# A state space block with adapters and experts on one Trainium2 core: the first additions of the states' products move from VectorE and GpSimd to two accumulating DMAs, and jobs change their places

## The reference

```python
h = x @ cond_W.T + b + 2 * (x @ A[idx]) @ Bm[idx]                    # cond: dense layer with an adapter
u, gate = split(h @ W_in.T)                                          # 2048 channels each
u = silu(causal_conv(u, 4 taps) + conv_b)
dt, Bm, Cm = split(u @ Wx.T, [64, 16, 16]); each rmsnorm * weight    # xp, ms
delta = softplus(dt @ Wdt.T + dt_bias)                               # dt
for t in tokens:                                                     # 2048 channels x 16 states
    state = exp(delta[t] * A) * state + delta[t] * u[t] * B[t]
    y[t] = sum_n state[n] * C[t][n]
x1 = x + ((y + u * D) * silu(gate)) @ W_out.T
h2 = x1 @ base_W.T + base_b + adapter2(x1)
w = top-2 softmax of h2 @ gate_w.T over 8 experts of rank 64
out = x1 + sum_e w_e * (h2 @ lora_A[e].T) @ lora_B[e].T
```

## Time and profile before

| | |
|---|---|
| median of 3 runs | 2556.78 us |
| the profiled execution | 2555.34 us, span 2553.6 us |
| PE busy | 2273.3 us (89%) |
| DVE busy | 2234.1 us (87%) |
| POOL busy | 2121.3 us (83%) |
| ACT busy | 1620.3 us (63%) |
| chain that ended last | PE 51%, DVE 22%, ACT 12%, issue 7%, POOL 7% |
| DMA | 350.05 MB, 137 GB/s in the mean, queue of SP 36.1% of 16 engines' span, of ACT 6.0% |

### The profile page before, as it was taken

One profiled execution on the slowest core, in us unless ns is written; L12 is line 12 of the kernel. 1 busy time (PEld: TensorE's weight loads), 2 busy tenths in 40 slices (PEclk: granted clock), 3 DMA queues, 4 the chain that ended last, 5 costly groups with the idle time before them and its releaser, 6 DMA issues.

```text
span 2553.6 us, 30492 instructions
## 1 busy us (share of the span) xinstructions
PE 2273.3 (89%) x10128; PEld 1918.1 (75%) x10128; DVE 2234.1 (87%) x2098; ACT 1620.3 (63%) x3768; POOL 2121.3 (83%) x1092
## 2 busy tenths in 40 slices
PE   7978898899879997999889997899978978787878
PEld 6867786688768886788768886788867766666767
DVE  1369797899989998999989998999989999999892
ACT  1367566776577766775667665776667765776550
POOL 0088787899889998999979998999979998999880
PEclk9989999899899998999999998999989998888989
DMA  6363443444345433544445433544426332432332
GB/s 209 125 212 100 115 142 119 151 142 139 119 171 155 140 133 105 197 149 140 125 142 168 148 126 116 177 160 136 135 70 215 116 108 91 169 120 90 116 104 89
DMA packets 132250, 350.05 MB, mean 137 GB/s; under 512 B 38573, under 2 KB 43181, under 8 KB 130621
## 3 DMA queue, kind: packets, MB, share of 16 engines
q1 hardware_dynamic: 109326, 296.19, 36.1%
q10 hardware_dynamic: 22768, 51.93, 6.0%
HBM read 337.04 MB, written 11.02 MB: 136 GB/s over the span
## 4 chain that ended last, share of the span: by engine, by line
PE 51%; DVE 22%; ACT 12%; issue 7%; POOL 7%; ACTq 1%; DMA 0%; SPq 0%; DVEq 0%; POOLq 0%
DVE scan L1241 12%; PE late L666 11%; PE ubank L584 10%; PE ubank L613 9%; ACT scan L1076 7%; DVE st L1253 5%; PE gbank L566 5%; POOL st L1464 3%; POOL st L1472 2%; PE scan L584 2%; PE small L640 2%; DVE ubank L1222 2%; PE gbank L630 2%; PE scan L566 1%; ACT ubank L937 1%
## 5 line engine op out<-in xcount | busy, mean ns | idle before, releaser
L1464 POOL TENSOR_TENSOR st<-w_sb,bc 128x1024 f32<-128x1024 f32 x512 | 1198.1, 2355 | 163.5 <-PE gbank L630 150.2
L1241 DVE TENSOR_TENSOR_SCAN scan<-scan,st 128x1024 f32<-128x1024 f32 x512 | 1156.5, 2285 | 40.1 <-POOL st L1464 22.7
L1076 ACT ACTIVATE scan<-delta,A_sb 128x255 f32<-128x255 f32 x2048 | 846.2, 459 | 0.0
L1472 POOL TENSOR_TENSOR st<-st 128x1024 f32<-128x1024 f32 x256 | 603.1, 2356 | 73.1 <-DVE st L1253 63.0
L584 PE MATMUL ubank<-h,wt 128*128 128x256 f32 x1712 | 445.2, 419 | 130.5 <-ACT qg L1155 125.7
L613 PE MATMUL ubank<-h,wt 128*128 128x256 f32 x2048 | 481.6, 390 | 41.5 <-ACT qg L1155 36.3
L584 PEld LDWEIGHTS ubank<-h,wt 128*128 128x128 f32 x1712 | 360.1, 213 | 208.4 <-ACT qg L1155 150.6
L1073 ACT ACTIVATE scan<-iota 128x4 f32<-128x4 f32 x512 | 86.8, 170 | 655.0 <-DVE st L1253 631.6
L613 PEld LDWEIGHTS ubank<-h,wt 128*128 128x128 f32 x2048 | 400.4, 196 | 103.7 <-ACT qg L1155 40.9
L1253 DVE TENSOR_TENSOR st<-scan,bc 128x1024 f32<-128x1024 f32 x384 | 453.7, 1207 | 0.0
L666 PE MATMUL late<-yg,wt 128*128 128x256 f32 x1792 | 410.5, 388 | 32.6 <-DVE x L1278 29.6
(11 more groups left out here) (217 smaller groups left out, 2253.8 us busy)
## 6 DMA issues: line engine op xcount, KB each, us to landing
wt<-in_W_in SPq DMA_DIRECT2D x256, 512.0 KB, 3.6
wt<-in_W_out SPq DMA_DIRECT2D x128, 512.0 KB, 3.4
wt<-in_cond_W SPq DMA_DIRECT2D x64, 512.0 KB, 3.6
bc<-bc_rows ACTq DMA_DIRECT2D x64, 512.0 KB, 6.6
wt<-G_tiles SPq DMA_DIRECT2D x32, 512.0 KB, 3.6
wt<-in_ffn_B SPq DMA_DIRECT2D x26, 512.0 KB, 3.4
xb<-in_x SPq DMA_DIRECT2D x8, 1024.0 KB, 5.6
x<-in_x ACTq DMA_DIRECT2D x28, 256.0 KB, 3.9
```

What stands on the lines that cost most here:

```text
L1076: last = fn(t[:, k, 1:T], delta[:, c, 1:T], ACT.Exp, scale=A_sb[:, col:col + 1])
L1241: v_.tensor_tensor_scan(Tps[q % 2][:, :], Tps[q % 2][:, :], x_, 0.0, ALU.mult, ALU.add).then_inc(scan_done, 1)
L1464: tt(st[:, n % ST_RING, :, :], w_sb[:, i % 2:i % 2 + 1, :].to_broadcast([P, NQ, T]), bc[:, 0, q * NQ:(q + 1) * NQ, :], ALU.mult).then_inc( ...
L1472: tt(st[:, n % ST_RING, :, :], st[:, n % ST_RING, :, :], st[:, (n - 1) % ST_RING, :, :], ALU.add).then_inc(add_done, 1)
```

## The change

It has two parts. In the first, quarter 1's product goes into the ring like the others, and POOL issues two DMAs that add: plane 1 += plane 0 as soon as the product of q = 1 is done, and plane 2 += plane 1 when that has landed and the product of q = 2 is done. POOL then adds plane 3 to plane 2 and folds as before. add_first is gone from DVE and one add from POOL. The ring has seven planes.

```diff
-ST_RING = 6
+ST_RING = 7
@@ vector
-                if q == 1:
-                    v_.tensor_tensor(Tps[1][:, :], Tps[1][:, :], cq, ALU.mult).then_inc(prod_done, 1)
-                else:
-                    v_.tensor_tensor(plane(n), Tps[q % 2][:, :], cq, ALU.mult).then_inc(mul_done, 1)
-
-            def add_first(i):
-                dve.wait_ge(prod_done, i + 1)
-                dve.wait_ge(mul_done, 4 * i + 1)
-                v_.tensor_tensor(plane(4 * i + 1), Tps[1][:, :], plane(4 * i), ALU.add).then_inc(mul_done, 1)
+                v_.tensor_tensor(plane(n), Tps[q % 2][:, :], cq, ALU.mult).then_inc(mul_done, 1)
@@ gpsimd
-                if q == 2 and i:
-                    pool.wait_ge(mul_done, 4 * i - 2)
-                if q == 1 and i >= 2:
+                if q == 2 and i >= 2:
                     pool.wait_ge(id_mm, i - 1)
+                if q == 3 and i:
+                    pool.wait_ge(acc_st[0], 16 * i)
+            def add_dma(i, k):
+                n = 4 * i + k
+                pool.wait_ge(mul_done, n + 1)
+                if k == 2:
+                    pool.wait_ge(acc_st[0], 16 * (i + 1))
+                pool.dma_start(st[:, n % ST_RING, :, :], st[:, (n - 1) % ST_RING, :, :], accum_op=ALU.add
+                               ).then_inc(acc_st[k - 1], 16)
@@ gpsimd, the loop over the chunks
+                last = i + 1 == CHUNKS
+                add_dma(i, 1)
                 for b, j in softplus_of(i - 1):
                     delta_add(b, j)
-                if i + 1 < CHUNKS:
+                if not last:
                     weight(i + 1)
-                    for q in range(3):
-                        dbu(i + 1, q)
-                add(i, 2)
+                    dbu(i + 1, 0)
+                    dbu(i + 1, 1)
+                add_dma(i, 2)
+                if not last:
+                    dbu(i + 1, 2)
+                    dbu(i + 1, 3)
                 add(i, 3)
                 fold(i)
-                if i + 1 < CHUNKS:
-                    dbu(i + 1, 3)
```

```diff
@@ u_chunks
-        if c <= 5:
+        if c <= 4:
             return [NC + 2 * (c - 1), NC + 2 * c - 1]
@@ half_job
-    if j < B and c in (1, 3, 5, 7, 8, 9):
-        return ("cond", j, {1: 0, 3: 1, 5: 2, 7: 4, 8: 5, 9: 7}[c])
+    if j < B and c in (3, 5, 7, 8, 9, 11):
+        return ("cond", j, {3: 0, 5: 1, 7: 2, 8: 3, 9: 5, 11: 7}[c])
@@ tensor
-                        for v in u_chunks(5):
+                        for v in u_chunks(4):
                             pe.wait_ge(u_done, v + 1)
...
                 ubank_free(i)
+                if small_job(i) and small_job(i)[0] == "xp":
+                    x_proj(small_job(i), range(NC - 1 if i >= NC else NC - 2, NC))
@@ scalar
                 fn_exp_table()
                 if i == 0:
-                    for m in range(4, KH):
-                        pro_cond(1, m)
+                    pro_cond(1, 4)
...
                     decay(i + 1, 0)
...
+                if i == 0:
+                    pro_cond(1, 5)
```

More of the change, by code:

```diff
@@ L103, in small_job @@
         return ("dt", b, c + 3)
-    if c in (6, 9) and j < B:
-        return ("cond", j, {6: 3, 9: 6}[c])
+    if c == 9 and j < B:
+        return ("cond", j, 4)
     if c in (10, 11):
         return (("lg", "wT")[c - 10], f, 0)
-    if c in (14, 15):
+    if b == LAST and c in (14, 15):
         return ("B", f, {14: 3, 15: 2}[c])
@@ L157, in takes_half @@
 def takes_half(i):
-    return late_job(i) if late_job(i) and late_job(i)[0] in ("g", "b2", "bias") else half_job(i)
+    if late_job(i) and late_job(i)[0] in ("g", "b2"):
+        return late_job(i)
+    return small_job(i) if small_job(i) and small_job(i)[0] == "bias" else half_job(i)
 def job_tiles(job):
@@ L362, in build @@
         scan_done = sem("scan_done")
-        prod_done = sem("prod_done")
         mul_done = sem("mul_done")
         add_done = sem("add_done")
+        acc_st = [sem(f"acc_st{i}") for i in range(2)]
         id_mm = sem("id_mm")
@@ L592, in h0_ready @@
                 else:
-                    pe.wait_ge(*emptied(("cond", b, 6)))
-                    pe.wait_ge(*emptied(("cond", b, 7)))
+                    for m in (4, 6, 7):
+                        pe.wait_ge(*emptied(("cond", b, m)))
             def ubank_free(i):
@@ L631, in sum_states, with x_proj @@
                 last.then_inc(id_mm, 1)
-            def x_proj(job):
+            def x_proj(job, cs):
                 b = job[1]
-                pe.wait_ge(u_done, NC * (b + 1))
-                for c in range(NC):
+                pe.wait_ge(u_done, NC * b + cs[-1] + 1)
+                for c in cs:
                     n = TILE_NO[("wx", b, c // 8)]
@@ L641, in x_proj @@
                               start=(c == 0), stop=(c == NC - 1))
-                last.then_inc(done_inc(job), 1)
+                if cs[-1] == NC - 1:
+                    last.then_inc(done_inc(job), 1)
             def mean_square(job):
@@ L721, in weights_b @@
             def weights_b(m, o):
-                return mm(o, sel[:, m * P:(m + 1) * P], wT[:, :], start=True, stop=True)
+                for e in range(2):
+                    pick = ident[0:E, 2 * m + e:2 * m + e + 1].to_broadcast([E, ER])
+                    last = mm(o[e * ER:(e + 1) * ER, :], pick, wT[:, :], start=True, stop=True)
+                return last
             def expert_out(f, m, o):
@@ L751, in run @@
                 elif kind == "xp":
-                    x_proj(job)
+                    x_proj(job, range(NC - 1 if i % NC == 12 and i >= NC else NC - 2))
                 elif kind == "ms":
```

137 lines of the change are left out of this document (71 added, 66 removed).

## The result

The changed kernel takes 2579.11 us, the median of 4 runs (2575.76 to 2580.49), against 2556.28 of the kernel before on the same chip: 1.009 times, with a 95% interval of 1.0072 to 1.0109. It is slower by 0.9%, where 2505 was forecast. The profiled executions have spans of 2578.7 and 2553.6 us, 25.1 apart.

What follows compares the result with a forecast made beforehand. Steady slots (first scan to next chunk's first scan, 17.56 us) were taken as bound by DVE, ACT, DVE, plus holes. 0 + 12 - 38 - 11 - 6.5 - 4 - 5 = -52.5 from 2556.78 gave 2505 us, range 2470 to 2650.

Steps and rivals of the forecast that it cites:

- part 2: GpSimd's add becomes two accumulating DMAs: its loop averages 17.35 us, under the 17.56 of a steady slot, so 0.
- part 3: Last slots and tail: GpSimd's longer loop and the last chunk's landing cost +12 us (ends 0 and +25).
- Part 1: The first add leaves DVE: it lies in ACT's shadow, so 0; the taps' wait on ACT becomes 1.5 us.
- Rival C: DVE's add does count, as the taps get their u chunk earlier; floor 2465 us; chance 0.08.
- e: Time POOL itself is busy issuing one adding DMA: taken as 1.0 us, ends 0 and 2.36.
- S: Time from POOL starting on an adding DMA's issue to its semaphore: taken as 6.6 us.
- close but covered: GpSimd's fold ends about 8.2 us into the next slot; PE needs it after 6.9 us of W_out and 0.9 of dt.
- Part 4: x_proj split and moved ahead: c = 13 falls 5.3 us, c = 14 1.0; -38 over six sequences (ends 0 and -49).
- Part 6: Evened placement, c = 1 to 7: PE's waits for a cond chunk at y_sum shrink, -5 us of 10.5.
- Part 5: First sequence: slot 6 -11 us, slots 0 and 1 -6.5, bias job's DMA issues moved to slot 12 -4.
- A: The round trips bind in each slot: slower than before from S = 7.4, 2585 us at 7.5, 2713 at 8; chance 0.33.

Runs made afterwards that it cites:

- p_only: The changed kernel with the adds of the kernel before (first add on DVE, two adds on GpSimd, ring of six planes); 2524.78 us, 0.988 of the kernel before.
- b_noadd: The kernel before without DVE's first add, so plane 0 is left out of y; 2542.31 us, 0.9958 of the kernel before.
- a_nobc: The changed kernel with the next sequence's broadcast loads of B and C cut to 8 columns of one state each; 2549.79 us, 0.998 of the kernel before.
- a_quiet: As a_nobc, and each weight load behind the first twelve is cut to its first 64 KB; 2519.51 us, 0.9855 of the kernel before.
- p_ms: p_only with the mean square ahead of expert_in on PE in chunk 13 of sequences 2 to 7; 2489.14 us, 0.9741 of the kernel before.
- p_wt: p_ms with the first dt projection ahead of the u chunk, and chunk 11's wT behind the sum and cond chunk; 2480.7 us, 0.9708 of the kernel before.

## Why the prediction was wrong

The sum was -52.5 and the spans differ by +25.1. The missing 77.6 us are in two of its steps: 43 in part 2 (the spans of the changed kernel and p_only, 55.8 apart, less the 12.9 of part 3) and 34 in parts 4 to 6 (-64.5 was said, and p_only's span is 30.7 under that of before).

**Part 1, DVE's add at 0: right.** The taps still start 8.63 us into the steady slot, with 1.58 us of wait on ACT (1.5 was said):

```profile
1736.29 1.54 DVE L1239 SCALAR_TENSOR_TENSOR ubank<-up,cw,ubank 128x256 f32<-128x256 f32 x3 [1.58 <-ACT ubank L948]
```

Alone it is worth 12 us (b_noadd), not 0 and not 157; in the changed kernel slot 11 of sequences 2 to 7 is 5.6 us shorter in all than in p_only, which keeps the add. The 43 us of part 2 are net of that. Rival C is out.

**Part 2, two round trips at 0: this step failed, with 43 us.** Not by its mean sizes. The issue took 0.88 us where e was 1.0, and the landings have a median of 5.4 (mean 6.0) where S was 6.6. (With the 0.3 us that the instruction behind an issue takes longer, e is 1.2.) By these the loop is shorter than I said, and in undisturbed slots it was hidden, at 17.55. What failed is that I put one S into the formula. The landings go from 4.4 to 11.8 us, and they grow with what moves beside them: by the packets in the trace, the 59 landings under 4.5 us had 76 KB of SP's loads beside them in the mean, and the 23 of 7.4 to 9 us had 1238 KB. At each c = 15 of sequences 1 to 7, beside the broadcasts, the first takes 10.0 to 11.8 and the second 7.0 to 9.5.

S + S is on GpSimd's loop, and a landing isn't hidden beyond what GpSimd does meanwhile (by the prediction's own terms with e = 0.88, 6.3 or 7.6 us for the first and 5.6 for the second), whatever the mean. Nor is it made up at once: GpSimd's own work is 16.8 us of a slot of 17.55 with a delta add. After the c = 0 shown above the first issue stands 15.5 us into its slot (7.7 is normal), then 10.2, 8.8 and 8.0 in the next three. The delay alone costs nothing more there: those three slots are as long as in p_only. It costs where further late landings meet it. In the fifth sequence landings of 9.8, 7.4 and 8.5 us in slots 5 and 6 push the first issue of slot 7 to 14.8 us; PE waits 5.1 us for the fold there and DVE 5.9 for PE, and that slot takes 23.6.

By place, changed kernel less p_only: c = 0 of sequences 2 to 7 16.6, their other slots 21.8 (scattered over slots of 18 to 24 us), the first sequence and what lies before it 4.5. The cover that I named was "close but covered", and it is what broke. By its own terms it was not there: the fold comes 14.5 + 1.2 + 6.6 + 3.6 - 17.56 = 8.3 us into the slot (8.2 was written), and PE needs it at 7.8. a_nobc and a_quiet show the cause: without the broadcasts and with light weight loads the cost is gone, and each of the two has a share. I had read the broadcasts' 6.6 us as a bound for S, and not as traffic that the new transfers would meet.

The estimate of 4.4 us, worked out in the prediction from the Trainium skill ("DMA: Bandwidth & Descriptors", section "Anatomy of one DMA — SWDGE (gpsimd) path"), agrees with the smallest landing, 4.4 here. Beside other traffic it was too low: 162 of the 256 landings took more than 5.0 us.

**Part 3, the last slots at +12: right in size, in part by luck.** Windows of the earlier trace rows against the changed kernel's, less what p_only has there (80.99 and 86.81): +6.9 and +1.0; the whole sequence 9.0, the tail 3.9, 12.9 in all. But of the 6.9, which I had put at 1.8 in each of five slots, 4.5 are at c = 0 of the last sequence, behind the seventh set of broadcasts (20.8 us, against 16.3 in p_only and 15.8 in a_nobc): that is part 2's failure again. In the tail the sum of the last chunk starts 2.5 us later than in p_only, near the 3 that were said, and 1.4 more are PE's last 64 records, which lose them to a lower clock. (The ends 0 and +25 of this part don't come out of its own formula either: it gives some +7 at S = 5.4 and +20 at 7.2.)

**Part 4, x_proj at -38: this step failed too; 15 came off at c = 13 and 14 of sequences 1 to 7, and 7 were lost again at c = 11.** The hole at c = 13 closed by 4.1, near the 5.3 that were said. expert_in started 4.4 us into the slot and not 3.0, since I had left the gate chunk of chunk 12 out of PE's queue there. But slot 14 rose, from 19.2 to 21.2 us in the mean of sequences 2 to 6, instead of falling by 1. The working took 6.9 us for u and gate behind the silu; they took 10.1 in the slot shown, since the u chunk ran at the lower clock level after 3.82 us of idle PE. The wait had moved, into a place where PE's clock was the price. The end of the range was real: in p_ms the two slots are 8.2 us a sequence shorter than before, 49 in six. And slot 11 rose from 18.8 to 20.5 in sequences 3 to 6 of p_only (19.5 in the changed kernel), with two cond chunks in it, one ahead of wT in the bank `late` and one behind it; p_wt gave 1.5 of it back by the order alone. Part 6 had no row for it and said -5: c = 8 did fall by 1.0 in each of sequences 2 to 6, but c = 2 and 3 rose by 0.33 each in sequences 3 to 7.

**Part 5, the first sequence at -21.5: right**, with -26 in p_only: slot 6 12.4 less, slots 0 to 3 7.8, the first slot of sequence 2 5.5. Some 2.4 of it were lost again, in slot 12, which the bias job's issues went to (17.2 to 18.7 us), and in the second slot of sequence 2 (17.2 to 18.2).

**The rivals.** The time came on the side of A, and A's place (both landings on GpSimd's loop, the add waiting) is where it was lost. But A needed S over 7.4 in each slot and made steady slots long. Steady slots stayed at 17.6, and 45 of 256 landings were over 7.4; that A's 2585 at S = 7.5 lies near the measured time is an accident. The case that came wasn't among mine: a mean that is harmless, and collisions in a sixth of the landings, whose delay stands for several slots and adds up where they follow each other. (A's 2713 doesn't add up from its terms: 127 slots of 19.6 are 2489, and with 135.9, 77, 12 and 7 that is 2721. Nothing rests on it.)
